# A fused layer of two expert stages around a scan: attention steps of sequences 0 and 1 at other tiles

## What is computed

```python
x = x + 0.5 * ffn(layernorm(x))      # 12 experts, each token uses its best 3
x = x + attn(layernorm(x))
x = x + 0.5 * ffn(layernorm(x))      # the same expert weights again

# ffn: gate_logits = x @ Wg; top 3 of 12, softmax over the three
#      h = gelu(x @ Wup[e] + bup[e]);  y = h @ Wdown[e] + bdown[e];  weighted sum
# attn: u = silu(x @ Wg + bg) * (x @ Wi + bi)
#       y = Cp * scan(u) + Dp * u      # scan with decay A, a convolution over time
#       y = layernorm_eps_1e-3(y) * gamma + beta
#       y = (silu(y @ Wfg + bfg) * (y @ Wfu + bfu)) @ Wfd + bfd;  return y @ Wo + bo
```

## Time and profile before

| | |
|---|---|
| time, median of 3 runs | 625.67 us (624.09 to 625.69) |
| span of the profiled execution | 623.9 us |
| TensorE busy | 560.0 us |
| ScalarE busy | 514.5 us |
| VectorE busy | 373.2 us |
| GpSimd busy | 416.4 us |

### The profile page before, as it was taken

How to read it: one execution, slowest core, us unless ns; L and a number is a source line. 1 busy time by engine, 2 the same in 40 slices (tenths; PEclk the granted TensorE clock), 3 DMA queues, 4 the chain that set the end, 5 groups by cost and what they waited for, 6 DMA issues and landing times.

```text
span 623.9 us, 17393 instructions
## 1 busy us (share of the span) xinstructions
PE 560.0 (90%) x4527; PEld 522.7 (84%) x4527; DVE 373.2 (60%) x1735; ACT 514.5 (82%) x1462; POOL 416.4 (67%) x424
## 2 busy tenths in 40 slices
PE   7559879999999999999899799998798799999995
PEld 6449779999999888878889688787698799999992
DVE  7947788653111577888865679987828532232224
ACT  3557777599998989899889699998589679998984
POOL 1074557677776777327677777777777777777770
PEclk9999988899999999999999799999799989999997
DMA  7996242343454343312255333332264532433264
GB/s 192 323 222 190 63 113 67 86 123 87 128 161 128 104 119 101 80 45 67 72 169 133 90 87 98 90 98 70 69 153 109 131 87 70 117 87 83 61 225 136
DMA packets 99127, 72.28 MB, mean 116 GB/s; under 512 B 13520, under 2 KB 91910, under 8 KB 99033
## 3 DMA queue, kind: packets, MB, share of 16 engines
q1 hardware_dynamic: 83032, 43.62, 25.5%
q0 software_dynamic: 13024, 26.11, 14.9%
q10 hardware_dynamic: 2976, 1.44, 0.9%
HBM read 37.08 MB, written 34.75 MB: 115 GB/s over the span
## 4 chain that ended last, share of the span: by engine, by line
PE 38%; DVE 15%; POOL 14%; issue 11%; DMA 11%; ACT 6%; SPq 3%; ACTq 1%; DVEq 1%; POOLq 0%
PE ps L1001 16%; PE ps L1014 15%; POOL YG L807 11%; DMA yk<-Ys,row 4%; DMA YG<-ys,SY 3%; ACT hT L1184 2%; POOL yk L818 2%; DVE YG L1698 2%; SPq L607 1%; PE ps L971 1%; DVE X L1311 1%; DVE st L1255 1%; DVE Ys L2037 1%; PE ps L961 1%; DMA xl<-xna,SG 1%
## 5 line engine op out<-in xcount | busy, mean ns | idle before, releaser
L1184 ACT ACTIVATE hT<-ps,BU 128x128 f32<-128x128 f32 x900 | 260.5, 390 | 52.8 <-PE ps L1001 42.0
L1014 PE MATMUL ps<-WD,hT 128*128 x1800 | 245.0, 281 | 18.8 <-DVE Ys L2037 18.7
L1001 PE MATMUL ps<-xT,WT 128*128 128x128 f32 x1800 | 248.7, 283 | 5.9 <-ACT xT L1174 3.0
L1014 PEld LDWEIGHTS ps<-WD,hT 128*128 128x128 f32 x1800 | 224.6, 196 | 22.2 <-issue 22.1
L1001 PEld LDWEIGHTS ps<-xT,WT 128*128 128x128 f32 x1800 | 228.5, 198 | 15.3 <-issue 11.7
L790 POOL DMA_INDIRECT xs<-XN,SX x144 | 146.6, 1018 | 64.6 <-issue 58.1
L807 POOL DMA_INDIRECT YG<-ys,SY x132 | 135.6, 1027 | 43.3 <-issue 35.3
L2037 DVE TENSOR_TENSOR Ys<-ps,BD 128x128 f32<-128x128 f32 x225 | 63.9, 288 | 165.9 <-PE ps L1014 158.5
L1067 ACT ACTIVATE WT<-WU 128x512 f32 x225 | 149.9, 667 | 7.0 <-DVE eW L1731 3.5
L818 POOL DMA_INDIRECT yk<-Ys,row x71 | 70.9, 999 | 21.7 <-issue 12.5
L777 POOL DMA_INDIRECT xl<-xna,SG x24 | 24.3, 1013 | 40.9 <-DMA xna<-XN 27.4
(11 more groups left out here) (366 smaller groups left out, 583.8 us busy)
## 6 DMA issues: line engine op xcount, KB each, us to landing
ys<-Ys SPq DMA_DIRECT2D x41, 256.0 KB
xl<-xs SPq DMA_DIRECT2D x94, 64.0 KB
xl<-xs SPq DMA_DIRECT2D x71, 66.0 KB
WU<-in_L_ffn_Wup_dram SPq DMA_DIRECT2D x12, 256.0 KB, 5.0
WD<-in_L_ffn_Wdown_dram SPq DMA_DIRECT2D x12, 256.0 KB, 5.2
YG<-yk SPq DMA_DIRECT2D x4, 768.0 KB, 7.6
xs<-XN,SX POOLq DMA_INDIRECT x144
YG<-ys,SY POOLq DMA_INDIRECT x132
```

The source lines that it names most:

```text
L1001: x = e.matmul(HB[i % 2][:, c * P:(c + 1) * P], WT[i % NW][:, c, :], xT[m % 2][:, j * P:(j + 1) * P], start=True, stop=True)
L1014: x = e.matmul(YB[i % 2][:, 0:D], hT[i % 3][:, c * P:(c + 1) * P], WDf[:, bass.ds(r + c * P, P)], start=(c == 0), stop=(c == C - 1))
L1184: x = e.activation(hT[i % 3][:, c * P:(c + 1) * P], HB[i % 2][:, c * P:(c + 1) * P], ACT.Gelu, bias=BU[:, bass.ds(b + c, 1)])
```

## The change

Fifteen lines of `CHAIN`, from C3 on, get new tile numbers for sequences 0 and 1. Sequence 0: A3 stands one tile sooner on TensorE, S3 and S3' one, A3 on ScalarE two, A4, A5, U5, A7, T, N, N', L and ScalarE's N four, K five. Sequence 1: C3 one, A3 two on TensorE, S3 and S3' one, A3 on ScalarE one, A4 two, and all that follow three. The numbers of the other sequences, the steps ahead of C3, `POOL` and the tables stay. `ring()` gives out the banks anew.

```diff
-    ("V", "C3", (15, 24, 31, 35, 61, 68, 74, 82)),
-    ("P", "A3", (18, 26, 33, 39, 63, 69, 77, 83)),
-    ("V", "S3", (19, 26, 33, 39, 65, 70, 78, 83)),
-    ("V", "S3'", (19, 26, 33, 39, 65, 70, 78, 83)),
-    ("A", "A3", (22, 28, 36, 42, 67, 72, 79, 84)),
-    ("PA", "A4", (25, 30, 37, 44, 68, 73, 80, 85)),
-    ("PA", "A5", (26, 32, 38, 45, 69, 74, 81, 86)),
-    ("V", "U5", (26, 32, 39, 45, 69, 76, 82, 86)),
-    ("PV", "A7", (28, 34, 40, 46, 72, 78, 83, 88)),
-    ("PA", "T", (29, 35, 42, 48, 73, 79, 84, 89)),
-    ("V", "N", (29, 35, 42, 49, 73, 79, 84, 89)),
-    ("V", "N'", (30, 36, 42, 50, 73, 80, 84, 89)),
-    ("PV", "L", (30, 37, 42, 50, 74, 80, 84, 89)),
-    ("A", "N", (31, 38, 44, 50, 75, 81, 85, 89)),
-    ("PV", "K", (33, 38, 44, 53, 75, 81, 86, 89)),
+    ("V", "C3", (15, 23, 31, 35, 61, 68, 74, 82)),
+    ("P", "A3", (17, 24, 33, 39, 63, 69, 77, 83)),
+    ("V", "S3", (18, 25, 33, 39, 65, 70, 78, 83)),
+    ("V", "S3'", (18, 25, 33, 39, 65, 70, 78, 83)),
+    ("A", "A3", (20, 27, 36, 42, 67, 72, 79, 84)),
+    ("PA", "A4", (21, 28, 37, 44, 68, 73, 80, 85)),
+    ("PA", "A5", (22, 29, 38, 45, 69, 74, 81, 86)),
+    ("V", "U5", (22, 29, 39, 45, 69, 76, 82, 86)),
+    ("PV", "A7", (24, 31, 40, 46, 72, 78, 83, 88)),
+    ("PA", "T", (25, 32, 42, 48, 73, 79, 84, 89)),
+    ("V", "N", (25, 32, 42, 49, 73, 79, 84, 89)),
+    ("V", "N'", (26, 33, 42, 50, 73, 80, 84, 89)),
+    ("PV", "L", (26, 33, 42, 50, 74, 80, 84, 89)),
+    ("A", "N", (27, 34, 44, 50, 75, 81, 85, 89)),
+    ("PV", "K", (28, 35, 44, 53, 75, 81, 86, 89)),
```

## The result

| | before | after |
|---|---|---|
| time, median (runs) | 624.88 us (622.39 to 625.69) | 635.64 us (632.63 to 638.82) |
| ratio, 95% interval | | 1.0158 (1.012 to 1.0196) |
| span of the profiled execution | 623.9 us | 630.8 us |
| second phase (tiles 0 to 46) | 129.9 us | 140.9 us |
| third, fourth phase | 141.3, 144.6 us | 140.4, 144.7 us |

What follows compares the result with a forecast made beforehand. TensorE's matmuls plus about 7 us of gaps bound the second phase, ScalarE nearly as full. Waits of 5.05 + 6.45 + 3.3 = 14.8 us, less 4.9, gave 9.9; the walk's 9 was taken: 634.7 us, range 627.5 to 639.5.

Steps and rivals of the forecast that it cites:

- No slack in the first chain: Tiles 17 to 22: S3, S3' of sequence 0 delay S1 of sequence 1; TensorE's wait at A1 grows from 0.8 to 3.45 us.
- A4 and A2 behind ScalarE's A3: Tiles 20 and 21: ScalarE does A3 of sequence 0 before A1's copy, so TensorE's A4 and A2 wait 1.2 us.
- Second pile-up: Tiles 24 to 29: VectorE reaches S1 of sequence 2 late and further TensorE waits follow; 6.45 us in all.
- The bank of A2's second half: Tile 27: A2's second half takes the group transpose's bank, emptied only behind the GELU; 1.0 us, between 0 and 1.0.
- Third part: Tiles 29 to 37: waits at C2 and A4 of sequence 2 and T of sequence 1; 3.3 us, bounds 0 to 4.
- The clock: Behind the waits of 3.45 and 3.8 us the granted clock may fall, costing 0 to 2 us each.
- rival (b): The clock falls behind both big waits: 12 us slower, 637.7 us; chance 0.09.
- The walk: Three engines followed tile by tile through tiles 17 to 38; TensorE ends tile 37 9.1 us later, 9 taken.
- Rival (a): Only the two chains of S1 behind S3 count, 2.7 + 3.6 us less later relief: 628 to 630 us; chance 0.18.
- Rival (c): VectorE is far enough ahead in tiles 18 and 25, new waits vanish: -3 us, 622.7 us; chance 0.08.
- (d): Tile numbers move but the order of events doesn't: within 1.5 us of 625.7; chance 0.09.
- GpSimd: Second phase: idle time before sequence 0's scatters shrinks from 19.4 us; over 5 us appears before sequence 2's.

Runs made afterwards that it cites:

- e4: The kernel before with only A3 (TensorE), S3 and S3' of sequence 0 one tile sooner; 946.04 us against 941.52, ratio 1.0049.
- e1: The changed kernel with S1 of sequences 1 and 2 one tile sooner, in front of S3; 943.99 us, ratio 1.0017 to the kernel before.
- e5: The changed kernel with 30 transposes of the identity in front of A1 of sequences 1 and 2; 945.53 us, ratio 1.0029 to the kernel before.
- e8: The changed kernel with S1 of sequences 1 and 2 one tile sooner and sequence 0's N, N', L, ScalarE's N and K at their old tiles; 633.97 us.
- e10: e8 with U5 of sequence 1 one tile later as well; 633.46 us, ratio 1.0132 to the kernel before.
- e13: The kernel before with the new tiles of sequence 1 alone, a repeat run; 942.23 us, ratio 1.0016.

## Why the prediction held

- **No slack in the first chain**: right, and the best step of it. Predicted at A1 of sequence 1: 3.45 us; measured 3.7. G waits 3.03 us for L1284 where about 3 was said, and e4 and e1 make and remove this wait by order alone.
- **A4 and A2 behind ScalarE's A3, 1.2 us**: right in size (1.3 us in step 20 of e1, a wait of 0.96 us in e5), though the changed kernel's trace shows no wait there, since TensorE runs slowly at that moment.
- **Second pile-up, 3.8 us at A1 of sequence 2**: 3.8 and 0.16 measured. A4 of sequence 1, 1.55 us: hidden by the clock in the same way, 1.69 us in e5. The bank of A2's second half: 0.35 us (0.46 in e5), inside the 0 to 1.0 given, and its value of 1.0 too high. The forecast's word for it, load of 24.2 against 19 us, fits e8, which takes 5.9 us off these tiles by taking steps out, where S1's place (e1) takes none off; that it is their amount alone is not shown. Measured, VectorE is busy for 17.3 us in these tiles before and for 23.1 after (19.6 and 24.2 in the forecast).
- **Third part, 3.3 us**: A4 of sequence 2 2.0 us (2.1 predicted), T of sequence 1 0.35 (0.9), small ones 1.2 (0.3).
- **The clock**: 0 to 2 us for each fall, beside the sum. Two falls came, 1.7 and 2.5 us of matmul time, the second over its bound. The sum of waits without them was 14.8; with them and without the waits that they hid, 16.2. Filling gives 0.7 us back, so rival (b), which added 3 us for them, was wrong in its size: it added what the next wait swallows, as its own sentence on the clock had said.
- **The walk**: the first matmul groups of tiles 21, 22, 25, 28, 29, 32, 34 and 38 start at 234.26, 239.73, 249.08, 260.50, 267.52, 276.53, 283.18 and 295.88. With the 3.3 us by which this execution's second phase begins sooner (185.02 and 188.33) that is 237.6, 243.0, 252.4, 263.8, 270.8, 279.8, 286.5 and 299.2. Up to tile 34 the walk is within 1.3 us of them, always early. Its end fell short by 1.8: there it gave back more than the small waits of tiles 29 to 37 let come (1.2 us measured, 0.3 in the sum). From tile 40 on the GELU groups stay 10.9 us behind those of before; nothing comes back, as was said.
- **Rival (a)**, only the two plain chains: its 628 to 630 us leave out ScalarE's queue and sequence 2's A4, which the rows show. **Rival (c)** fell with G's wait, and **(d)** too.
- **GpSimd**: idle time before sequence 0's scatters 12.9 us (19.4), 9.1 us before sequence 2's, where over 5 was named. Those of sequence 0 start 6.2 us sooner, not some 8, and those of sequence 1 3.5 us later, not at about the old time. The second phase lasts 140.9 us where some 139 were said, and the third begins at 325.9, past the 322 that would have spoken against.
- The forecast met 635.64 us within 1 us. Part of this is luck: its 9 us stand against 11.0 us of phase and 10.8 us between the medians, so it was some 2 us short, and 0.8 us of that was made up because the median before fell from 625.67 to 624.88 us with the fourth run. The sum of the waits, 9.9 us, was nearer than the walk's 9 that was taken.

## What to carry to other kernels

Before steps are moved closer in a software pipeline, look for chains in the trace whose consumer already waits a little (0.61 us). The 3.1 us of statistics that were put in front of such a chain cost 4.0 us (e4), 5.1 with ScalarE's step behind them. And count each engine's work per tile in the stretch that gets more: here it exceeded the bottleneck's, and three further arrangements (e1, e8, e10) moved the lateness from step to step and didn't remove it. Where such a wait brings a clock fall, look first at removing the wait: in tiles 19 to 23 that gave 3.5 us (e1), keeping the clock up 0.5 (e5).

## What of the hardware was unexpected

**The same program at 941 us.** On two of the chips the kernel before took 941 us (on one of them 933 to 951 in 54 runs), elsewhere 621 to 631. VectorE and ScalarE are as busy there as elsewhere (374.0 and 514.8 us in e13), GpSimd too (413.4), but TensorE has some fourteen stretches like this one, in tiles 50 and 51 of e13, with gaps between its matmuls in which it waits for nothing that the profile shows:

```profile
502.42 0.37 PE L1014 MATMUL ps<-WD,hT 128*128 x1 [0.98 <-issue]
503.83 0.60 PE L1014 MATMUL ps<-WD,hT 128*128 x2 [1.04 <-issue]
505.27 0.37 PE L1014 MATMUL ps<-WD,hT 128*128 x1 [0.84 <-issue]
...
514.54 0.37 PE L1001 MATMUL ps<-xT,WT 128*128 128x128 f32 x1 [1.07 <-issue]
515.94 0.37 PE L1001 MATMUL ps<-xT,WT 128*128 128x128 f32 x1 [1.03 <-issue]
```

```profile
520.00:540.00 20.00, 3.27 (x11) 2.31 (x11) 1.44 (x8) 0.60 (x1) 15.17 (x16) 0.50 0.20 50
```

Single matmuls follow each other 1.4 us apart in these rows; the window behind them has eleven in 20 us, and there the granted clock is 0.50. Why isn't known; the DMA engines' share of 0.20 in it is below the 0.28 of that whole execution. Most stand at the same tiles in every kernel there (tiles 50, 51 and 56 in all of them; tile 51 alone takes 31 to 46 us there, 2.0 elsewhere), so they go with a place in the program.

**Clock falls that cost little.** 4.2 us of longer matmuls at the lower clock were worth 0.7 us of tile steps, because ScalarE, behind which TensorE would have waited, was busy throughout both stretches. With 30 transposes of the identity in each wait (3.4 us) the granted clock behind it was 1.00 (e5), where behind the empty waits it was 0.57 and 0.52.
